# Stepped reads instead of stepped writes in PSUM, first denominators ahead of V's last column, one plane copy issued by ScalarE

## What is computed

```python
qkv = conv1x1(x, w_qkv)                         # 384 channels: per head 8 of q, 8 of k, 8 of v
agg = conv(conv(qkv, w_dw, groups=384, pad=2), w_pw, groups=48)   # 5x5 depthwise, then 8x8 blocks
qkv = concatenate([qkv, agg], axis=1)
q, k, v = relu(qkv[:, :, :8]), relu(qkv[:, :, 8:16]), qkv[:, :, 16:]
v  = pad(v, one more row of ones)
vk = einsum('bhdn,bhen->bhde', v, k)
out = einsum('bhde,bhen->bhdn', vk, q)
out = out[:, :, :-1] / (out[:, :, -1:] + EPS)   # the denominators: sum of k over pixels, times q
x = x + conv1x1(out, w_proj)
# second layer: theta, phi from x; softmax(theta^T phi / 8); times x; conv1x1 with w_fuse; plus x
```

## Time and profile before

| What | Value |
|---|---|
| Median of three runs | 64.95 us |
| The profiled execution | 64.65 us |
| Its span in the trace | 62.9 us |
| TensorE matmuls (PE) busy | 56.2 us, 89% |
| TensorE weight loads (PEld) busy | 42.4 us, 67% |
| VectorE (DVE) busy | 39.2 us, 62% |
| ScalarE (ACT) busy | 23.0 us, 37% |
| GpSimd (POOL) busy | 21.2 us, 34% |
| Chain that ended last | PE 59%, ACT 12%, DVE 10%, DMA 6%, issue 4%, SPq 4% |

### The profile page before, as it was taken

How to read it: one execution, slowest core, us unless ns; L and a number is a source line. 1 busy time by engine, 2 the same in 40 slices (tenths; PEclk the granted TensorE clock), 3 DMA queues, 4 the chain that set the end, 5 groups by cost and what they waited for, 6 DMA issues and landing times.

```text
span 62.9 us, 2287 instructions
## 1 busy us (share of the span) xinstructions
PE 56.2 (89%) x990; PEld 42.4 (67%) x990; DVE 39.2 (62%) x97; ACT 23.0 (37%) x53; POOL 21.2 (34%) x32
## 2 busy tenths in 40 slices
PE   2998989999979999989929999999999999889940
PEld 2767979679958476637604757599997579576830
DVE  3693069989788473003005989495885569896450
ACT  0832349703477440003600003360200519995300
POOL 4991000288999999999000000000000000000000
DMA  0784351078935689999992000000000000000342
GB/s 0 222 198 129 99 169 42 10 166 226 243 84 128 169 212 231 185 239 231 198 153 34 0 0 10 0 0 10 0 0 0 0 0 5 0 0 0 105 146 83
DMA packets 5945, 5.86 MB, mean 93 GB/s; under 512 B 2080, under 2 KB 5424, under 8 KB 5936
## 3 DMA queue, kind: packets, MB, share of 16 engines
q1 hardware_dynamic: 4624, 4.06, 28.1%
q10 hardware_dynamic: 1024, 1.25, 7.5%
q0 software_dynamic: 288, 0.41, 2.9%
HBM read 1.19 MB, written 0.52 MB: 27 GB/s over the span
## 4 chain that ended last, share of the span: by engine, by line
PE 59%; ACT 12%; DVE 10%; DMA 6%; issue 4%; SPq 4%
PE bank L793 16%; PE bank L781 7%; PE bank L957 6%; ACT pr L548 6%; DMA wpair<-wnext 6%; PE bank L760 5%; PE bank L828 3%; PE bank L838 3%; PE bank L804 3%; SPq L374 3%; PE bank L980 3%; PE bank L1021 3%; PE bank L818 3%; DVE xp L598 2%; ACT planes L477 2%
## 5 line engine op out<-in xcount | busy, mean ns | idle before, releaser
L793 PE MATMUL bank<-planes,wpair 64*32 64x256 f32 x288 | 10.0, 393 | 0.6 <-DMA wpair<-wnext 0.4
L793 PEld LDWEIGHTS bank<-planes,wpair 64*32 64x32 f32 x288 | 5.6, 105 | 3.7 <-issue 1.6
L760 PE MATMUL bank<-wqkv_t,xp 128*128 128x128 f32 x48 | 7.3, 310 | 0.3 <-DVE wqkv_t L602 0.3
L760 PEld LDWEIGHTS bank<-wqkv_t,xp 128*128 128x128 f32 x48 | 6.7, 220 | 1.2 <-issue 0.6
L781 PE MATMUL bank<-planes,wlast 32*32 32x256 f32 x288 | 6.6, 396 | 0.2 <-DVE conv L630 0.2
L781 PEld LDWEIGHTS bank<-planes,wlast 32*32 32x32 f32 x288 | 4.1, 103 | 1.6 <-issue 0.5
L477 ACT ACTIVATE planes<-bank 128x512 f32<-128x512 f32 x6 | 3.7, 643 | 2.2 <-PE bank L771 1.2
L746 PE MATMUL bank<-warm 128*128 128x256 f32 (+1 forms) x8 | 3.5, 588 | 1.2 <-DVE warm L563 1.2
L468 ACT ACTIVATE toks<-bank 128x512 f32<-128x512 f32 x4 | 2.4, 600 | 5.5 <-PE bank L760 5.5
L481 ACT ACTIVATE conv<-bank 128x512 f32<-128x512 f32 x3 | 1.8, 600 | 6.9 <-PE bank L793 6.9
L548 ACT ACTIVATE pr<-bank,nmx 128x256 f32<-128x256 f32 x8 | 3.7, 476 | 1.8 <-DVE nmx L708 1.7
(11 more groups left out here) (109 smaller groups left out, 105.9 us busy)
## 6 DMA issues: line engine op xcount, KB each, us to landing
planes<-planes SPq DMA_DIRECT2D x10, 180.0 KB, 3.8
xs<-in_x ACTq DMA_DIRECT2D x2, 256.0 KB, 3.1
rq<-q_relu SPq DMA_DIRECT2D x4, 128.0 KB, 4.5
wpair<-wnext POOLq DMA_DIRECT2D x8, 48.0 KB, 2.8
out<-ys SPq DMA_DIRECT2D x3, 128.0 KB, 1.7
planes<-planes ACTq DMA_DIRECT2D x2, 180.0 KB, 4.0
rq<-conv SPq DMA_DIRECT2D x2, 128.0 KB, 4.5
rq<-conv ACTq DMA_DIRECT2D x2, 128.0 KB, 4.8
```

The source lines that it names most:

```text
L760: last = nc.tensor.matmul(tokens_bank(kind, pair)[:, a], xp[:, pair, a, :], wqkv_t[:, kind, :], start=True, stop=True)
L793: last = nc.tensor.matmul(bank[32 * quad:32 * (quad + 1), 2 * h + j, 0:NPIX], wpair[rows, kind, j, quad, u, :], window(rows, plane_set(kin ...
```

## The change

1. `by_pixel` now writes each phase's product into 128 neighbouring floats of the bank, and the two `tokens` copies read the bank with a step instead, so that `toks` is as before. This touches six bank copies: K's two, Q's first and V's first on ScalarE, Q's second and V's second on VectorE.
2. `WPW_T` moves from bank 6 to bank 2, and TensorE's wait for `wpw_out` ahead of `to_planes(K)` goes.
3. `denominators(0)`, with its two waits, goes ahead of V's last column.
4. Q's fourth twin copy is no longer issued by SyncE, but by ScalarE after V's two plane copies; it has a semaphore of its own, `twin_act_q`, for which TensorE waits ahead of Q's pairs.

```diff
-        WARM, WQKV_T, W_V, WPW_T = 3, 4, 5, 6
+        WARM, WQKV_T, W_V, WPW_T = 3, 4, 5, 2
...
         def tokens_bank(kind, pair):
-            return bank[:, TOK[kind][pair], :].rearrange("p (m a) -> p a m", a=PHASES)
+            return bank[:, TOK[kind][pair], :].rearrange("p (a m) -> p m a", a=PHASES)
+
+        def tokens_kept(kind, pair):
+            return toks[:, kind, pair, :].rearrange("p (m a) -> p m a", a=PHASES)
...
             sp.wait_ge(plane_dve[Q], 2)
-            twins(Q, 1)
+            sp.dma_start(*twin_copy(Q, 1)).then_inc(twin_moved[Q], 16)
...
-                nc.scalar.activation(toks[:, kind, pair, :], bank[:, TOK[kind][pair], :], ACT.Copy).then_inc(tok_out[kind][pair], 1)
+                nc.scalar.activation(tokens_kept(kind, pair), tokens_bank(kind, pair), ACT.Copy).then_inc(tok_out[kind][pair], 1)
...
             plane(V, 1)
+            act.dma_start(*twin_copy(Q, 3)).then_inc(twin_act_q, 16)
             conv_first_rounds(K, 1)
...
-                nc.vector.tensor_copy(toks[:, kind, pair, :], bank[:, TOK[kind][pair], :]).then_inc(tok_out[kind][pair], 1)
+                nc.vector.tensor_copy(tokens_kept(kind, pair), tokens_bank(kind, pair)).then_inc(tok_out[kind][pair], 1)
...
                 for a in range(PHASES):
-                    last = nc.tensor.matmul(tokens_bank(kind, pair)[:, a], xp[:, pair, a, :], wqkv_t[:, kind, :],
-                                            start=True, stop=True)
+                    last = nc.tensor.matmul(bank[:, TOK[kind][pair], a * P:(a + 1) * P], xp[:, pair, a, :],
+                                            wqkv_t[:, kind, :], start=True, stop=True)
...
             weights(2)
-            pe.wait_ge(wpw_out, 1)
             to_planes(K)
...
             pe.wait_ge(pair_moved[Q], 16 * QUADS)
-            pe.wait_ge(twin_moved[Q], 16 * QUADS)
+            pe.wait_ge(twin_moved[Q], 16 * 3)
+            pe.wait_ge(twin_act_q, 16)
             convolve_pairs(Q, range(0, 3))
...
             by_token(K, 1, TR_K, tr_k_mm)
+            pe.wait_ge(rq0_moved, 16 * QUADS)
+            pe.wait_ge(ks_out, 2)
+            denominators(0)
             pe.wait_ge(wconv_pool[V], 4)
             pe.wait_ge(conv_act, 2)
             pe.wait_ge(conv_dve, 2)
             convolve_last_column(V)
-            pe.wait_ge(rq0_moved, 16 * QUADS)
-            pe.wait_ge(ks_out, 2)
-            denominators(0)
```

More of the change, by code:

```diff
@@ L170, in conv_attention_kernel @@
         twin_moved, twin_act = [sem(f"twin_moved{k}") for k in range(KINDS)], sem("twin_act")
+        twin_act_q = sem("twin_act_q")
         pair_act = sem("pair_act")
```

## The result

| What | Before | After |
|---|---|---|
| Median of the runs | 64.81 us (64.53 to 65.05, four) | 68.68 us (67.76 to 71.06, four) |
| Ratio | 1 | 1.044, 95% interval 1.0375 to 1.0504 |
| The profiled execution, its span | 64.65, 62.9 us | 67.95, 66.0 us |

The change makes the kernel slower by 4.4%, where I forecast 64.8 us with 64.0 to 65.6 as the range. Executions that count as disturbed, among them those of 69.41 and 71.06 us, are in the medians of this document and not in its ratios.

The account below looks back on a forecast made before the run. TensorE was taken as bound by two instruction refills from 27.27 to 36.89, by its own work behind. Terms 0.00 - 0.02 + 0.00 + 0.00 + 0.1 - 0.25 + 0.05 = -0.12 us gave 64.8 us, range 64.0 to 65.6.

Parts of the forecast that it names:

- the limit that I had named: K's transposes: the second needs K's second `toks` copy, ending at 8.80, so dropping the wait saves only 0.02 us.
- the predicted place: Second "issue" stall: same instruction along the stream, with two or three matmuls of V's last column left.
- ScalarE was not late: Rival on the twin's issue running to 22.1, or stepped reads costing half as much again: 65.3 to 65.7 us, 9%.
- That wait is free too: Denominators ahead of V's last column: a 0.45 us query wait still ends ahead of the refill at 32.99; price 0.00.
- term (a): Refill that starts at 27.27: +0.8 us for V's fourth twin ahead, -0.65 for earlier-drained work, taken as +0.1.
- The refill is late: Rival: V's fourth twin stands ahead of the refill of 27.27, nothing drained; +0.8 us, 65.75, packet after 30.85; 10%.
- the cover for Q's twins: ScalarE's twin was to land at 23.6, while Q's pairs start at 24.49: 0.9 us of cover, no price.
- Term (c): Refill ending in the 0.25 us stall at 27.27 meets more of `rq`: +0.05 us, bounds 0 and 0.25.
- Term (b): Refill at 32.99: V's last twin lands 0.65 us earlier, gathers behind it clear sooner; -0.25 us.

Follow-up runs that it names:

- only_reads: The kernel before with only the stepped `toks` reads (ordered product writes) and without the wait for `wpw_out`; 65.01 us, ratio 1.0059.
- quiet_wait: The kernel before with TensorE also waiting for the second reciprocals ahead of the first projected sums, while no DMA runs; 67.93 us, one run.
- two_twins_held: The kernel before with V's last two twins issued by SyncE behind its gathers; 70.37 us, one run.
- only_first_sums: The kernel before with only the first denominators and their two waits moved ahead of V's last column; 66.74 us, ratio 1.013.
- late_query: The kernel before with TensorE's query wait ahead of V's last column and the last `rq` copy issued behind V's first two twins; 65.12 us, one run.
- all_but_twin: The whole change without Q's fourth twin on ScalarE, so parts 1 to 3 on the kernel before; 67.87 us.
- late_query_early_wait: late_query with TensorE's query wait one call earlier, between the two pairs of convolved K's transposes; 68.05 us, one run.
- only_twin: The kernel before with only Q's fourth twin issued by ScalarE; 65.66 us, ratio 1.0138.
- change_padded: The whole change plus two idle products of 16 columns (8 instructions) ahead of K's transposes; 67.45 us.
- only_wait: The kernel before with only TensorE's wait for the queries moved ahead of V's last column, no product moved; 65.76 us, ratio 1.0131.
- first_sums_padded: only_first_sums plus two idle products of 16 columns (8 instructions) ahead of K's transposes; 67.49 us, ratio 1.034.
- eight_more: The kernel before with eight idle products of 16 columns (32 instructions) ahead of K's transposes; 65.14 us, one run.
- gathers_after_sums: only_first_sums with the four gathers of convolved queries issued only when the first denominators are done; 65.20 us, ratio 1.008.
- sums_after_third: The kernel before with the first denominators and their waits behind the first third of V's last column; 65.23 us, ratio 1.0041.

## Why the prediction was wrong

**What held.** The products keep their time, the copies cost 602 ns for 600, and `only_reads` is 0.2 us above before by the medians and 0.4 by the ratio. The first transpose lost its wait for `wpw_t`, and the next one stood 0.27 us for the second `toks` copy, the limit that I had named. The stalls are refills of 256 instructions, and the second one stands in the predicted place, behind the 94th of V's last 96. ScalarE was not late: it issued the twin at 19.86 in 0.52 us, beside its plane copy, and the next copy of K began at 20.86.

**The step that failed: "That wait is free too".** I priced the wait for the queries at 29.09 to 29.54 at nothing, since TensorE would come to the end of its block ahead of 32.99 either way. That holds the refill's arrival fixed and moves TensorE against it. In fact the refill hangs on TensorE's own progress: while TensorE stands at a semaphore early in the block, the refill doesn't come (`quiet_wait`, on empty queues). My premise that it is asked for when the block is entered does not fit `two_twins_held` either. The wait of 0.45 us was sized right (0.51, 0.64 and 0.67 us measured); its effect was not. TensorE went on behind it at 30.00 in after and 29.72 in `only_first_sums`, where before passed the place at 29.09. By that the refill was asked for 0.6 to 0.9 us later, which is an estimate, for no trace shows the request; it met the gathers, issued from 29.1 us on in after and from 28.7 in `only_first_sums`, and its packet came 1.6 us (after) or 2.5 us (`only_first_sums`) later. In the sum this is term (a), the refill of 27.27: I put it at +0.1 us, and TensorE went on 1.79 us later. The rival "The refill is late" had the right place, and its sign came true (a packet behind 30.85), but with a wrong cause and size: it put +0.8 us on V's fourth twin ahead of the refill, and holding back two twins did not bring the packet forward.

The Trainium skill (Runtime: NRT & Kernel Launch, section Instruction fetch mechanics) says that the next page is fetched while the current one runs. This case agrees for an engine that runs, and for one that stands at the 54th instruction of the block or so (`late_query`). It disagrees for one that stands earlier: with the 2.06 us wait of `quiet_wait` the packet ran 3.8 us behind the entry, for 1.4 without it.

**A term that wasn't there: the clock.** Behind the 2.02 us pause the granted clock was 0.50 from 35.0 to 38.4, which costs 1.2 us, more than a third of the loss. It doesn't follow from the pause alone: `all_but_twin` had it after 3.12 us of pause, `late_query_early_wait` and `two_twins_held` had it at pauses of 2.70, `only_first_sums` not after 3.13 (32 matmuls of V's pairs took 1.15 us behind it), `quiet_wait` not after 2.06. Nor is it needed: the fourth execution of after, at a mean clock of 0.999, took 67.76 us, as long as the profiled one at 0.972.

**Part 4, priced 0.00.** It measured 0.8 us in `only_twin`. I took SyncE's issues at their old duration, 0.65 us each. But some are longer. Of before's, 19.56 to 21.19 lies over the refill's packet of 19.24 to 20.81, and 24.59 to 26.05 over the one of 24.21 to 25.67; that isn't the whole cause, since two `rq` issues of `only_twin` took 1.09 and 1.03 us from 20.93 to 23.09, where no such packet ran. In after too the head start is lost:

```profile
18.45 1.95 SPq L378 DMA_DIRECT2D planes<-planes  x2
20.45 0.85 SPq L389 DMA_DIRECT2D planes<-planes  x1
21.40 2.80 SPq L393 DMA_DIRECT2D rq<-q_relu  x4
24.24 3.40 SPq L378 DMA_DIRECT2D planes<-planes  x4
```

SyncE begins `rq` at 21.40 for 21.92, and the last of it lands at 29.95 for 29.54; V's twins at 33.0 for 32.59. And the cover for Q's twins that I put at 0.9 us was for the one that moved. It landed at 22.47 in after, but at 25.61 in `change_padded`, where TensorE waited for it. The third, still on SyncE, landed at 24.62 in after. TensorE, ready at 24.13, stood 0.58 us and began Q's pairs at 24.71 (24.49 in before); the profile calls that "issue", the landing is the nearest event. Kernels with all of Q's twins on SyncE had such waits too (0.41 us in `only_wait`, 0.59 in `late_query`), so it can't be put down to part 4 alone. Term (c), the stall in Q's pairs, was 0.13 us more in after (0.38 for 0.25) and 0.28 in `only_twin`, above its 0.05 and just past its bound of 0.25. Term (b), -0.25, was based on gathers clearing sooner; they landed at 34.7 and 35.0, later than before's 34.2 and 34.6.

**What stays open.** Where in the block the request is made; why `first_sums_padded` is slow in most of its executions and why `change_padded` had a late packet without a wait for the queries; why kernels with the sums first have both 65 and 67.5 us (that TensorE meets the queries in some executions and waits in others fits the two profiles, 65.68 without a wait and 67.54 with one, and is argued, not shown); what decides whether the clock falls; the 0.8 us of `only_wait` and the 0.4 us of `only_reads`.

## What to carry to other kernels

Where stalls called "issue" stand at equal distances along an engine's stream, as here at 256 instructions, suspect refills: count the instructions of a stretch, weight loads and semaphore instructions with them, and shift them by a few idle ones as `eight_more` does. In such a block a wait early on may not be swallowed by the stall at its end, since it can delay the refill too, and worst here where bulk copies were about to be issued. So move a wait later in the block or hold those copies back (`gathers_after_sums`, `sums_after_third`), and price a slack only after asking whether what it waits for depends on the engine itself.

## What was not expected of the hardware

- A refill didn't come while TensorE stood at a semaphore near the start of a block: 3.8 us from entry to packet on empty queues with a wait of 2.06 us (`quiet_wait`), 1.4 us without the wait.
- With busy queues, a wait of 0.64 us made the packet 2.5 us later (`only_first_sums`); from the packet's start to TensorE's going on it took 2.4 to 3.1 us in the kernels of the table.
- SyncE's four `rq` issues took 2.6 us in before, 2.8 in after and 3.5 in `only_twin`, and beginning them 0.5 to 1.0 us earlier brought the last copy no earlier (29.95 and 29.78 for 29.54).
- Writing or reading PSUM with a step of four floats cost nothing that shows: a median of 275 ns for the products either way, 602 ns for 600 in ScalarE's copies.
